# Second attention of a two-layer transformer: its first turns in a new order, two routed sums added earlier, and the second layer's routing moved from VectorE to GpSimd

## What is computed

```python
xn = layernorm(x)                                  # layer 0
x = x + causal_softmax_attention(xn, 16 heads) + gelu(xn @ W1) @ W2 + top2_of_8_experts(xn, F=512)
xn = layernorm(x)                                  # layer 1
h = rmsnorm(xn) * norm_w
q, k = rope(h @ Wq.T), rope(h @ Wk.T);  v = h @ Wv.T       # 8 heads of 32
beta, ig, og = sigmoid(gates of h)                 # one number per token and head
M = M * beta + ig * scale * outer(k, v)            # per token, state 32 x 32
y = (q @ M) * og
logits = xn @ router_w + router_b                  # routing of the second layer
top_w, sel = top_k(logits, 2); gates = softmax(top_w)
x = x + y @ Wout.T + bout + sum of the two chosen experts' gelu(xn @ w1 + b1) @ w2 + b2   # F=1024
```

## Time and profile before

| | |
|---|---|
| Median of 3 runs | 1636.55 us (1634.8 to 1641.53) |
| The profiled execution | 1643.91 us, span 1642.2 us |
| Mean granted TensorE clock | 0.981 of full speed |
| TensorE busy | 1543.8 us (94%) |
| VectorE busy | 865.9 us (53%) |
| ScalarE busy | 733.1 us (45%) |
| GpSimd busy | 717.8 us (44%) |
| Chain that ended last | TensorE 68%, VectorE 9%, issue 8%, GpSimd 8%, DMA 3%, ScalarE 3% |

### The profile page before, as it was taken

How to read it: one execution, slowest core, us unless ns; L and a number is a source line. 1 busy time by engine, 2 the same in 40 slices (tenths; PEclk the granted TensorE clock), 3 DMA queues, 4 the chain that set the end, 5 groups by cost and what they waited for, 6 DMA issues and landing times.

```text
span 1642.2 us, 32345 instructions
## 1 busy us (share of the span) xinstructions
PE 1543.8 (94%) x10802; PEld 1184.8 (72%) x10802; DVE 865.9 (53%) x2424; ACT 733.1 (45%) x1923; POOL 717.8 (44%) x815
## 2 busy tenths in 40 slices
PE   6989989999989999999997799998999999999997
PEld 3545445555547999998665467767999899999996
DVE  6777897887822444442577778874222122222220
ACT  4544545565551323323656566644333343334332
POOL 3122235666532555553810467763333433333332
PEclk9999999999999999999998999999999999999999
DMA  8533325445305343444631385367333333333331
GB/s 271 128 113 93 89 79 99 93 103 99 87 4 237 106 114 111 114 115 120 207 103 65 103 222 104 79 102 293 58 54 53 51 57 53 55 59 58 53 55 23
DMA packets 154639, 167.60 MB, mean 102 GB/s; under 512 B 84820, under 2 KB 132816, under 8 KB 151408
## 3 DMA queue, kind: packets, MB, share of 16 engines
q1 hardware_dynamic: 129936, 128.15, 30.8%
q0 software_dynamic: 24544, 37.38, 10.5%
HBM read 104.10 MB, written 44.45 MB: 90 GB/s over the span
## 4 chain that ended last, share of the span: by engine, by line
PE 68%; DVE 9%; issue 8%; POOL 8%; DMA 3%; ACT 3%; SPq 1%; DVEq 0%; POOLq 0%; ACTq 0%
PE PS L1660 23%; PE PS L1678 22%; POOL SLOT L954 6%; PE PS L1517 4%; DVE PS L1980 3%; PE PS L1453 3%; PE PS L1502 3%; PE PS L1481 2%; PE PS L1463 2%; PE PS L1543 2%; PE PS L1634 2%; PE PS L1588 2%; POOL arena L1056 1%; POOL arena L1062 1%; ACT arena L1178 1%
## 5 line engine op out<-in xcount | busy, mean ns | idle before, releaser
L1660 PEld LDWEIGHTS PS<-arena 128*128 128x128 f32 x3408 | 398.3, 193 | 16.2 <-DVE arena L2201 4.9
L1660 PE MATMUL PS<-arena 128*128 128x128 f32 x3408 | 405.3, 276 | 3.5 <-DVE arena L2201 3.5
L1678 PE MATMUL PS<-arena 128*128 x1704 | 392.3, 379 | 0.0
L1678 PEld LDWEIGHTS PS<-arena 128*128 128x128 f32 x1704 | 312.4, 190 | 39.7 <-issue 0.2
L1980 DVE CUSTOM_DVE_ANT_0 PS<-PS,arena 128x512 f32<-128x512 f32 (+3 forms) x512 | 235.4, 523 | 46.0 <-PE PS L1481 41.9
L995 POOL DMA_INDIRECT out<-arena x71 | 111.6, 1573 | 296.4 <-ACT arena L1272 274.6
L1262 ACT ACTIVATE arena<-PS,arena 128x128 f32<-128x128 f32 x568 | 161.8, 368 | 138.3 <-PE PS L1660 135.9
L2226 DVE COPY arena<-arena 128x8 f32 x71 | 12.5, 175 | 348.3 <-ACT arena L1262 326.9
L928 POOL TENSOR_SCALAR_AFFINE_SELECT arena<-arena 128x256 f32<-128x256 f32 x256 | 99.5, 412 | 206.5 <-ACT arena L1178 206.1
L981 POOL DMA_INDIRECT arena<-XN,arena x142 | 145.8, 1027 | 100.4 <-PE PS L1645 40.6
L1178 ACT ACTIVATE arena<-PS 128x512 f32<-128x512 f32 (+1 forms) x256 | 166.3, 705 | 49.5 <-PE PS L1502 39.2
(11 more groups left out here) (248 smaller groups left out, 2031.4 us busy)
## 6 DMA issues: line engine op xcount, KB each, us to landing
arena<-FD SPq DMA_DIRECT2D x32, 512.0 KB
arena<-in_w SPq DMA_DIRECT2D x16, 1024.0 KB
SPL<-arena SPq DMA_DIRECT2D x32, 384.0 KB, 2.6
arena<-SPL SPq DMA_DIRECT2D x64, 192.0 KB
XN<-arena SPq DMA_DIRECT2D x16, 512.0 KB, 3.0
arena<-SPL SPq DMA_DIRECT2D x64, 128.0 KB
arena<-SUM SPq DMA_DIRECT2D x16, 512.0 KB, 6.8
arena<-in_x SPq DMA_DIRECT2D x8, 512.0 KB, 6.8
```

The costliest lines, as they stand in the source:

```text
L1660: ins = pe.matmul(o, m.now[i % 2][:, c * F + 128 * f:c * F + 128 * f + 128], m.xt[i % 2][:, 128 * c:128 * c + 128], start=(c == 0), stop=( ...
L1678: ins = pe.matmul(to, m.hT[i % len(m.hT)][:, 128 * c:128 * c + 128], m.WD[:, bass.ds(e * (nf * 256) + c * 256, 256)], start=(c == 0), stop ...
```

## The change

Five things are done.

1. **Routed sums early.** `combine` 6 and 7 move from VectorE to GpSimd and come right after `sums` 6 and 7, behind product 28; `shared_add` of these blocks now waits for them, and `stats` waits for `shared_add`. `sum_load` 7 moves from behind product 33 to behind product 22. `stats`, `root`, `scale` and `norm` of block 6 come one product earlier, `root` 6 thereby ahead of the last gelu.
2. **The last normalized block on GpSimd.** `norm` 7 is four GpSimd instructions (L1056 of the changed kernel), ahead of `open` 0.
3. **First turns.** A list START replaces turns -1 and 0 of the loop. `project_qk` 0 writes bank 1, so that `project_qk` 1 need not wait for `rope` 0; the logits of block 7 go to bank 1 as well; `logitsT` 6, `picks` 6, `decay` 1 and others come later.
4. **Routing on GpSimd.** The one-hot masks, C and a constant (`spread`, six instructions and a cast), the tiles' experts (`place_tiles`, eight) and the positions (`place_rows`, three, and `place_pick` 0 and 1, five each) are GpSimd steps; comparisons become a subtraction and a comparison with zero, and sums over eight or seven experts become pairwise adds. VectorE keeps the copies of the counts, the running sums and the gate weights. The steps stand in turns 3 to 6, one kind in each place.
5. **Scatters** begin in turn 7 instead of turn 6 and are three in every turn.

In the changed kernel GpSimd's lines are `sums` L1037, `combine` L1048, `norm1` L1056, `gates` L1067, `open` L1076 and L1082, `spread` L1107 to L1116, `place_tiles` L1123 to L1136, `place_rows` L1141 to L1145, `place_pick` L1151 to L1159, `scatter` L964.

```diff
...
-    28: "sums:6 logits_copy:3 logitsT:3",
+    28: "sums:6 combine:6 sums:7 combine:7 logits_copy:3 logitsT:3",
...
-    34: "logits_copy:4 xa:5 logitsT:4 combine:6 stats:6",
-    35: "logitsT_copy:4 picks:4 logits:5 logits_copy:5 root:6",
...
+    34: "logits_copy:4 xa:5 logitsT:4 root:6",
...
+START = ("project_qk:0 logitsT:6 project_val:0 rope:0 value:0 logitsT_copy:6 scale:7 rope_add:0 norm:7 open:0 project_qk:1 turn:0 "
+         "keys:0 turned:0 rope:1 project_val:1 value:1 rope_add:1 xt:7 decay:1 xa:7 open:1 project_qk:2 "
+         "affinity:0 logits:7 picks:6 weigh:0 decay_load:2 logits_copy:7 gates:1:0")
...
     (2, "sums_copy"): "gates:1:3",
-    (5, "rope_add"): "gates:1:4",
+    (3, "decay"): "picks:7",
+    (7, "rope_add"): "gates:1:4",
+    (3, "open"): "spread",
+    (4, "project_out"): "count",
+    (4, "rope_add"): "route:15",
+    (4, "open"): "route:16",
+    (5, "open"): "route:17",
+    (5, "decay_load"): "place_tiles",
+    (6, "decay_load"): "place_rows place_pick:0 place_pick:1",
+    (6, "rope_add"): "route:14",
...
-    route = iter([("route", p) for p in range(14, 20)] + [("scatter", i, (k,)) for i in range(NT) for k in range(2)])
-    out = []
-    for n in range(-1, NT):
+    scatters = iter([("scatter", i, (k,)) for i in range(NT) for k in range(2)])
+    out = list(steps(START))
+    begun = set(out)
+    for n in range(1, NT):
         for kind, ahead in TURN if n < NB else LATE:
             out += steps(AMONG.get((n, kind), ""))
             if kind == "route":
-                for _ in range(0 if n < 3 else 2 if n < 6 else 3 if n % 3 else 2):
-                    out += [s for s in [next(route, None)] if s]
-            elif 0 <= n + ahead < NT and not (kind in ("decay", "decay_load") and n + ahead < 2):
+                for _ in range(3 if n >= 7 else 0):
+                    out += [s for s in [next(scatters, None)] if s]
+            elif 0 <= n + ahead < NT and (kind, n + ahead) not in begun and (kind, n + ahead) != ("decay", 0):
                 out.append((kind, n + ahead))
         if n % 8 == 1 and n > 8:
             out.append(("store_sums", n // 8 - 1))
         if n == NT - 2:
-            assert next(route, None) is None
+            assert next(scatters, None) is None
...
-            return 0 < b < 6
+            return b > 0
+
+        def qk_bank(n):
+
+            return 1 if n == 0 else 0
+
+        PICKED1 = 29 + 3 * NB
+        ROUTED1 = PICKED1 + 5
...
+                if b < 6:
+                    pool.wait_ge(sh_added, 4 * b + 4)
...
+            def norm1(b):
+                pool.wait_ge(normed, 16 + 2 * b + 2)
+                pool.wait_ge(xn_out[b % 2], 64 + 16 * (b // 2))
+                pool.wait_ge(turned, 16 + 2 * b - 2)
+                for j in range(4):
+                    i = 4 * b + j
+                    ins = pool.tensor_scalar(xn1[b % 2][:, j, :], ACC[:, i, :], RS[:, i:i + 1], NB1[:, i:i + 1], ALU.mult, ALU.add)
+                ins.then_inc(xn_made)
...
+            def spread():
+                r = RR[1]
+                pool.wait_ge(r_step, PICKED1)
+                pool.tensor_copy(r.IXF, r.IX).then_inc(r_place)
+                i8 = iota8.unsqueeze(1).to_broadcast([128, NT, 8])
+                pool.wait_ge(r_place, 1)
+                for n, oh in enumerate((r.OH1, r.OH2)):
+                    pool.tensor_tensor(oh, i8, r.IXF[:, :, n:n + 1].to_broadcast([128, NT, 8]), ALU.subtract).then_inc(r_place)
+                    pool.wait_ge(r_place, 2 + 2 * n)
+                    pool.tensor_scalar(oh, oh, 0.0, None, ALU.is_equal).then_inc(r_place)
+                pool.wait_ge(r_place, 5)
+                pool.tensor_tensor(r.C, r.OH1, r.OH2, ALU.add).then_inc(r_place)
+                pool.tensor_scalar(r.NTB, iota128.unsqueeze(1).to_broadcast([128, 8, 32]), 1.0, None, ALU.min).then_inc(r_place)
+            def place_tiles():
+                r = RR[1]
+                tend, n8 = r.n8[3], r.n8
+                pool.wait_ge(r_step, ROUTED1)
+                cmp = r.CMP[:, 0:NTILE, :]
+                pool.tensor_tensor(cmp, tend[:, 0:7].unsqueeze(1).to_broadcast([128, NTILE, 7]), iotaT[:, 0:NTILE].unsqueeze(2).to_broadcast([128, NTILE, 7]), ALU.subtract).then_inc(r_place)
+                pool.tensor_tensor(n8[4], tend, n8[0], ALU.subtract).then_inc(r_place)
+                pool.wait_ge(r_place, 8)
+                pool.tensor_scalar(cmp, cmp, 0.0, None, ALU.is_le).then_inc(r_place)
+                pool.wait_ge(r_place, 9)
+                pool.tensor_scalar(n8[4], n8[4], 128.0, None, ALU.mult).then_inc(r_place)
+                pool.wait_ge(r_place, 10)
+                pool.tensor_tensor(cmp[:, :, 0:3], cmp[:, :, 0:3], cmp[:, :, 3:6], ALU.add).then_inc(r_place)
+                pool.wait_ge(r_place, 12)
+                pool.tensor_tensor(cmp[:, :, 0:2], cmp[:, :, 0:2], cmp[:, :, 2:7:4], ALU.add).then_inc(r_place)
+                pool.wait_ge(r_place, 13)
+                pool.tensor_tensor(cmp[:, :, 0:1], cmp[:, :, 0:1], cmp[:, :, 1:2], ALU.add).then_inc(r_place)
+                pool.wait_ge(r_place, 14)
+                pool.tensor_copy(TEXI[:, 0:NTILE].unsqueeze(2), cmp[:, :, 0:1]).then_inc(r_expert)
+            def place_rows():
+                r = RR[1]
+                oth, cum = r.B, r.cum.rearrange("p (e i) -> p i e", e=8)
+                pool.tensor_tensor(oth, cum, r.AE.rearrange("p e i -> p i e"), ALU.subtract).then_inc(r_place)
+                pool.wait_ge(r_place, 15)
+                pool.tensor_tensor(oth, oth, r.n8[4].unsqueeze(1).to_broadcast([128, NT, 8]), ALU.add).then_inc(r_place)
+                pool.wait_ge(r_place, 16)
+                pool.tensor_tensor(oth, r.C, oth, ALU.add).then_inc(r_place)
+            def place_pick(n):
+                r = RR[1]
+                oh, k = (r.OH1, r.OH2)[n], 17 + 4 * n
+                pool.wait_ge(r_place, 17)
+                pool.tensor_tensor(oh, oh, r.B, ALU.mult).then_inc(r_place)
+                pool.wait_ge(r_place, k + 1)
+                pool.tensor_tensor(oh[:, :, 0:4], oh[:, :, 0:4], oh[:, :, 4:8], ALU.add).then_inc(r_place)
+                pool.wait_ge(r_place, k + 2)
+                pool.tensor_tensor(oh[:, :, 0:2], oh[:, :, 0:2], oh[:, :, 2:4], ALU.add).then_inc(r_place)
+                pool.wait_ge(r_place, k + 3)
+                pool.tensor_tensor(oh[:, :, 0:1], oh[:, :, 0:1], oh[:, :, 1:2], ALU.add).then_inc(r_place)
+                pool.wait_ge(r_place, k + 4)
+                ins = pool.tensor_copy(POS[:, n, :].unsqueeze(2), oh[:, :, 0:1])
...
-                pe.wait_ge(r_pick, layer + 1)
+                pe.wait_ge(*((r_pick, 1), (r_place, 6))[layer])
...
-                    pe.wait_ge(dk_mul, 4)
+                    pe.wait_ge(roped, 1)
...
             def project_qk(n):
                 i = ORDER1[n]
-                if n:
+                if n >= 2:
                     pe.wait_ge(roped, n)
-                else:
+                elif n == 0:
                     pe.wait_ge(nw_done, 4)
                 for c in range(2):
-                    ins = pe.matmul(ps(0, 0, 512), xnT[:, c, 128 * i:128 * i + 128], QKW[:, c, 0:512], start=(c == 0), stop=(c == 1))
+                    ins = pe.matmul(ps(qk_bank(n), 0, 512), xnT[:, c, 128 * i:128 * i + 128], QKW[:, c, 0:512], start=(c == 0), stop=(c == 1))
...
-                elif kind == "route" and a[0] == 15:
+                elif kind == "count":
...
+                    if layer:
+                        dve.wait_ge(r_place, 7)
+                        dve.wait_ge(r_counted, 1)
...
+                if b >= 6:
+                    dve.wait_ge(combined, b + 1)
...
             def stats1(b):
-                dve.wait_ge(combined, b + 1)
+                if b < 6:
+                    dve.wait_ge(combined, b + 1)
+                else:
+                    dve.wait_ge(sh_added, 4 * b + 4)
```

90 lines of the change are left out of this document (48 added, 42 removed).

## The result

| | kernel before | changed kernel |
|---|---|---|
| Median, first rounds (20 runs each) | 1635.9 us (1631.1 to 1641.68) | 1642.25 us (1635.33 to 1647.2) |
| Ratio | | 1.004, 95% interval 1.0028 to 1.0053 |
| Ratio in two later sets of rounds (12 runs of the changed kernel each) | | 1.0026 (1.0008 to 1.0044) and 1.0007 (0.9993 to 1.002) |
| Profiled execution | 1643.91 us, span 1642.2 | 1641.42 us, span 1639.6 |
| GpSimd busy | 717.8 us | 744.8 us |

The account below looks back on a forecast made before the run. TensorE was taken to bound the steady last turns, with waits on other engines in the turns before. Terms 3.6 - 6.8 + 5.9 + 0 - 3.0 = -0.3 us, off the median 1636.55, gave 1636 us, range 1622 to 1648.

Parts of the forecast that it names:

- Start, +3.6: End of the shared FFN to turn 2: weigh 0 +5.9 us, turn 1 at 4.5, turn 2 unchanged; +3.6 us.
- Turns 3 to 5, -6.8: Second attention, turns 3 to 5: routing leaves VectorE, 25 us against 31.76; -6.8 us.
- Turns 6 to 8, +5.9: Turns 6 to 8: GpSimd becomes the longest queue, 13 to 17 us from open 7 to open 8; +5.9 us.
- Turn 9, 0: Turn 9 keeps its 10.04 us, a low clock of 0.67 included; 0 us.
- Turns 10 to 14, 0: Turns from 10 on stay bound by TensorE; three scatters add 0.4 us to a GpSimd 75% busy; 0 us.
- The end, -3.0: End of the turns: of TensorE's 3.23 us wait for the slot table some 0.5 stays; -3.0 us.
- Slower rival: GpSimd's queue: small steps at 1.5 times their price add 9.1 us, ending at about 1645.5; chance 0.22.
- Faster rival: Turns 3 to 8 and the end: GpSimd's slack hides spread and place_tiles, some -13 us, hence 1623.5; chance 0.29.
- No change: Turns 6 to 9: pauses come from weight loads and stay, turns 6 to 8 within 1 us; about 1634; chance 0.10.

Follow-up runs that it names:

- after_root_late: The changed kernel with root 6 behind the last gelu again; 0.9988 of the kernel before.
- after_both: The changed kernel with root 6 behind the last gelu and norm 7 on ScalarE; 0.9957 of the kernel before.
- before_again: The kernel before, unchanged, profiled a second time; that execution took 1633.93 us.
- before_store_late: The kernel before with the first 1 MB store of sums in turn 15 instead of turn 9; 0.9996 of the kernel before.
- route_apart: The kernel before with parts 4 and 5 of the change, place_pick 1 behind open 8 and scatters from turn 8; 0.992 of the kernel before.
- before_loads_apart: The kernel before with the seven early 1 MB weight loads in every second turn from turn 6; 0.9985 of the kernel before.
- The two halves: The kernel before with only parts 1 to 3 of the change, 1.0043 of the kernel before, and with only parts 4 and 5, 0.9994.
- start_only: The kernel before with parts 1 to 3 of the change; 1.0043 of the kernel before.

## Why the prediction was right or wrong

The forecast was -0.3 us, the first rounds say +6.4. Two steps of the prediction failed.

The first is a term put at nothing: "Turns from 10 on stay TensorE's". Turns 10 to 14 lost 6.0, 5.2 and 3.9 us in the three profiles of the changed kernel, waiting for decay loads.

The second is the yardstick. The terms were read from an execution that "lies 7.4 above the median of the runs", and their sum was then taken off the median, as if the change left alone what made that execution long. Part of it was in turns 6 to 9, which the change rebuilt: 37.41 us in that profile, 28.98 and 29.75 in two others with the same order there. Against the first profile the sum came out, -0.7 us from the table load to weigh 31, by luck: the errors of the six terms are +0.2, -1.6, -1.5, -3.0, +6.0 and -0.5. Against the second it is +5.3. How much of the +6.4 each of the two steps has is not shown.

- **Start, +3.6.** Right against the profile it was read from: weigh 0 +6.1 (I had 5.9), turn 1 at 4.49 (4.5), turn 2 at 9.10 (9.1), so +3.8 at weigh 2 (+1.3 against the second profile, whose own start was longer). The parts were mis-sized: norm 7 took 5.01, not 3.7, since a scan of 2.28 (at 864.79) ran beside one of its steps, and the root cost 4.2 by `after_root_late`, not 2.6, since I had not counted what the pause does to the clock of the products behind it. That the sum came out all the same is luck in part: the rest of the start, which `after_both` shows alone, gained 2.3 us at weigh 0.
- **Turns 3 to 5, -6.8.** Right; -8.4. Turn 4 took 8.99 instead of 10.2.
- **Turns 6 to 8, +5.9.** Right in mechanism and near in size, +4.5: 15.0 us from open 7 to open 8, against 13 to 17, and turn 8 at 16.3. The +5.9 took the upper end of its own 32 to 33.3 for weigh 8; 31.82 was measured. Against the second profile the term is +10.3.
- **Turn 9, 0.** Wrong: 7.04 or 7.05 instead of 10.04, in all three profiles of the changed kernel, at a granted clock of 1.00. The low clock of 0.67, which the prediction kept, stands only in those profiles of the kernel before that have the two unnamed waits ahead of it; `before_again` has 7.42 us at 1.00.
- **Turns 10 to 14, 0.** Wrong, as said. I weighed the three scatters against GpSimd's busy share and never asked what else a turn there depends on. The profile of before shows it: the DMA share is 1.06 in turn 11, and one scan waits for its decay load, though TensorE is never idle for it:

```profile
971.84 2.29 DVE L2376 TENSOR_TENSOR_SCAN arena<-arena 128x1024 f32<-128x1024 f32 x1 [0.81 <-DMA arena<-FD]
```

  A load that is just in time is a bound that the next change can meet. The prediction named contention of loads only as a reason for no change. Why the loads come late more in some executions than in others stays open.
- **The end, -3.0.** The working gave 3.23 less 0.5, -2.7. TensorE's wait for the slot table fell from 3.23 to 0.88 us, -2.35, in these two executions; in `before_again` it was 1.3 without the change, in `before_store_late` 0.91:

```profile
1104.14 0.43 PE L1646 MATMUL PS<-arena 71*128 71x71 f32 x2 [0.88 <-DMA arena<-SLOT]
```

- **Slower rival.** Its place was right, its price not. Steps of 32 to 213 elements took 0.25 to 0.58 us; `place_tiles` ran 6.7 us with its first step held by a scan (2.95), some 4.9 with my price of 1.2 for that step, against my 5.4 to 5.6. Turns 6 to 8 gave +4.5 us, not the 15 (5.9 + 9.1) that it needs.
- **Faster rival.** Fell with turn 8, though -8.4 of its 10.7 came. `route_apart` shows what it needed: the queue taken apart, and the start left as it was, 0.992.
- **No change.** Turns 6 to 8 didn't stay within 1 us of the first profile, and its reason doesn't hold for turn 8: the pause stays when the weight load leaves that turn (`before_loads_apart`).

The two halves show where the sign comes from: the start is a loss of 0.4% that the routing, at 0.9994, doesn't repay. Only part of that loss is there at weigh 2 (+3.6 us in `start_only` against the first profile, +1.1 against the second); in its one profile turns 10 to 14 lose more than that (43.84 against 37.70 in the second).

## What to carry to other kernels

Cut a change into its halves and time each: here most terms agreed with the forecast, while the sign hung on terms that vary between executions by more than the sum. Profile the kernel before twice ahead of a forecast: an execution that is longer than the median has something in it that the median may lack, here 8.4 us in turns 6 to 9. When a step moves ahead of another on an engine, ask what the engine behind does in the pause: a 2.7 us pause cost TensorE 1.6 us more in its next products, at a granted clock of 0.70. Work that is moved to an idle engine belongs where its queue has a whole turn of slack; the same steps in two turns instead of one were worth 3 to 5 us in turns 6 to 9, and 0.3% in the one comparison within a set of rounds.

## What was not expected of the hardware

- In turns 3 to 8 of the changed kernel every GpSimd step that began while a scan of 1024 elements ran took 2.3 to 3.0 us, whatever its kind: a cast of 256 elements 2.32 (another cast of 256 took 0.40 alone), an add of 128 elements 2.32 (0.46 in place_pick 0). A scan that began under a GpSimd step was held in turn: the one at 929.63 took 2.81. I had it only for an open. The Trainium skill, page "SBUF — State Buffer", section "Who interferes with whom", has this exclusion for a VectorE step with two inputs in SBUF beside a GpSimd step that reads SBUF. The cast, with one input, agrees with it: the two inputs are asked of VectorE's step alone.
- A decay load of 512 KB landed 12.90 us after issue in the changed kernel, where the median of such loads is 6.0 and turns of 7 us follow each other.
- The kernel before had medians of 1635.9, 1638.84, 1642.91, 1646.94, 1649.02 and 1646.71 us in six sets of rounds, 0.8% apart. The last five ran on four chips; the third and the fourth set, on the same one, are 4 us apart. Within a set the runs spread by about as much as the sets.
